# A two-pass attention layer: float32r parts for the query and key projections, 17-column values, and three steps of the slot plan moved

## The reference, cut to what matters

```python
qk = x @ W_attn + b_attn                       # queries and keys, 256 -> 512
y  = causal_attn(q, k, v=x)                    # first pass
e  = v[1:] - y[:-1]                            # second pass: values are what y missed
k2 = x[:-1] @ W_k2 + b_k2
y2 = causal_attn(q[1:], k2, e), one row of zeros put ahead
x  = layernorm(x + (y @ W_proj + b_proj) + (y2 @ W_proj + b_proj))
x  = layernorm(x + ffn(x))                     # experts touch only the first 512 rows
```

## Time and profile before

| | us |
|---|---|
| median of 3 runs | 2620.78 (2616.14 to 2626.06) |
| the profiled execution | 2615.51 |
| its span | 2613.8 |
| PE busy | 2477.4 (95%) |
| DVE busy | 2123.0 (81%) |
| ACT busy | 1763.8 (67%) |
| POOL busy | 1397.3 (53%) |

### The profile page before, as it was taken

One profiled execution on the slowest core, in us unless ns is written; L12 is line 12 of the kernel. 1 busy time (PEld: TensorE's weight loads), 2 busy tenths in 40 slices (PEclk: granted clock), 3 DMA queues, 4 the chain that ended last, 5 costly groups with the idle time before them and its releaser, 6 DMA issues.

```text
span 2613.8 us, 64356 instructions
## 1 busy us (share of the span) xinstructions
PE 2477.4 (95%) x19286; PEld 1215.6 (47%) x19286; DVE 2123.0 (81%) x9392; ACT 1763.8 (67%) x3388; POOL 1397.3 (53%) x2214
## 2 busy tenths in 40 slices
PE   3999999999999999999999999999999999999997
PEld 1444444444444444444444444444444444444444
DVE  2788888888888888888888888888888888888755
ACT  0377777677777766777777677777776777777652
POOL 2355555555555555555555555555555555555432
PEclk8699999999999999999999999999999999999999
DMA  5455555565555546555555565555556555554211
GB/s 96 87 105 87 93 94 101 98 116 103 104 92 95 101 91 111 108 106 95 93 96 97 103 116 103 101 91 94 103 90 115 104 107 95 92 100 86 67 53 52
DMA packets 187779, 251.18 MB, mean 96 GB/s; under 512 B 26769, under 2 KB 103193, under 8 KB 187417
## 3 DMA queue, kind: packets, MB, share of 16 engines
q1 hardware_dynamic: 187440, 247.07, 51.7%
HBM read 74.60 MB, written 16.78 MB: 35 GB/s over the span
## 4 chain that ended last, share of the span: by engine, by line
PE 79%; issue 7%; DVE 6%; ACT 5%; POOL 3%; SPq 1%; DMA 1%; ACTq 0%; POOLq 0%; DVEq 0%
PE score_t L627 22%; PE out_t L588 21%; PE misc L692 14%; PE score L638 9%; PE misc L727 5%; PE turn L670 5%; DVE junk L820 3%; ACT prob L498 2%; PE score L775 1%; ACT y_t L530 1%; PE misc L714 1%; POOL prob L422 1%; DVE resid L871 1%; PE score L791 1%; DVE max_cols L820 1%
## 5 line engine op out<-in xcount | busy, mean ns | idle before, releaser
L820 DVE CUSTOM_DVE_ANT_0 junk<-score,mask_rows 128x384 bf16<-128x384 f32 (+3 forms) x3584 | 1689.6, 514 | 378.5 <-PE score L638 374.8
L498 ACT ACTIVATE prob<-score_t 128x512 f32<-128x512 f32 x2560 | 1403.6, 598 | 614.4 <-PE score_t L627 609.6
L422 POOL TENSOR_SCALAR_AFFINE_SELECT prob<-prob 128x512 f32<-128x512 f32 (+1 forms) x1280 | 726.5, 569 | 1046.2 <-ACT prob L498 1046.1
L627 PE MATMUL score_t<-stack_q,stack_k 50*128 50x128 f32 (+5 forms) x4096 | 1052.7, 364 | 45.0 <-ACT prob L498 34.0
L638 PE MATMUL score<-stack_k,stack_q 48*128 48x512 f32 (+3 forms) x4096 | 1040.1, 352 | 9.8 <-DMA stack_q<-part_l 7.7
L627 PEld LDWEIGHTS score_t<-stack_q,stack_k 50*128 50x128 f32 (+1 forms) x4096 | 600.7, 185 | 778.2 <-ACT prob L498 673.3
L588 PE MATMUL out_t<-prob,value 128*32 128x512 f32 (+3 forms) x8192 | 711.3, 442 | 0.0
L638 PEld LDWEIGHTS score<-stack_k,stack_q 48*128 48x128 f32 x4096 | 607.8, 188 | 27.2 <-DVE max_cols L820 16.0
L692 PE MATMUL misc<-x_t,wq 128*128 128x512 f32 x512 | 285.4, 641 | 60.8 <-DMA bias<-L_attn_b_proj 31.3
L820 DVE DVE_READ_ACCUMULATOR2_ANT max_cols<- 128x1 f32 x4096 | 337.2, 82 | 0.0
L588 PEld LDWEIGHTS out_t<-prob,value 128*32 128x32 f32 x8192 | 187.5, 108 | 312.3 <-issue 215.1
(11 more groups left out here) (83 smaller groups left out, 1233.7 us busy)
## 6 DMA issues: line engine op xcount, KB each, us to landing
stack_k<-part_h SPq DMA_DIRECT2D x512, 128.0 KB, 4.2
stack_k<-part_l SPq DMA_DIRECT2D x256, 128.0 KB, 4.5
stack_q<-part_h SPq DMA_DIRECT2D x256, 128.0 KB, 4.1
x_t<-x_turned SPq DMA_DIRECT2D x32, 512.0 KB, 9.5
x_in<-L_attn_x SPq DMA_DIRECT2D x32, 512.0 KB, 14.1
stack_q<-part_l SPq DMA_DIRECT2D x128, 128.0 KB, 5.1
resid<-L_attn_x SPq DMA_DIRECT2D x32, 512.0 KB, 6.2
layer_out<-resid SPq DMA_DIRECT2D x31, 512.0 KB, 5.4
```

The lines of the kernel that those rows point to most:

```text
L422: e.affine_select(out=view, in_=view, compare_op=ALU.is_ge, fill=0.0, base=-unit_parts(unit)[1], pattern=[[0, runs], [0, cut], [1, P]], ch ...
L498: e.activation(prob[pair % RING][:, slot % 2 * 512:slot % 2 * 512 + 512], score_t[time % KEY_DEPTH][:, :], ACT.Exp, scale=1.0 / np.sqrt(HE ...
L627: done = e.matmul(score_t[now % KEY_DEPTH][:, col:col + n], keys[rows, pair, kb * P:(kb + 1) * P], stack_q[b % 2][rows, pair, kb * P:token ...
L820: e.tensor_tensor_reduce(junk[count % JUNK][:, 0:n], score[number % MAX_DEPTH][:, col:col + n], mask, 1.0, -3e38, ALU.add, ALU.max, max_co ...
```

## The change

Four things are changed, and nothing of what is computed:

1. The six pieces are made of float32r parts. The weights are loaded as float32 into space that `prob` uses later, and DVE splits them at the start into high and low parts (four operations), for which PE's first piece waits. x is loaded into one float32 tile `x_full`, and POOL splits it, per 128 channels, into high and low at slots 4 and 7 of place 6 (four operations a batch, after the mask and the piece's own split in each slot). Each L692 matmul becomes three float32r matmuls (high by high, low weights by high x, high weights by low x). There is one `x_t` instead of two, so the split of a batch waits until the last piece of the batch before is made, and the load of the next x waits for the split.
2. Value tiles are 17 columns wide instead of 32, and each L588 matmul writes 17 rows of its strip. `out_t` is cleared once at the start, so that the rows that are never written are defined.
3. ACT copies turned y one slot earlier, at (1, 3) and (2, 3), behind the `heads_t` copy of that slot.
4. The norm is applied at slots 3, 5, 7 and 9 of place 5, and the output's DMA goes from (6, 0) to (6, 1).

The core of the diff:

```diff
-        wq = sb("wq", [P, halves, 2 * halves, P])
-        wk2 = sb("wk2", [P, halves, halves, P])
+        wq = [sb(f"wq_{part}", [P, halves, 2 * halves, P], F32R) for part in "hl"]
+        wk2 = [sb(f"wk2_{part}", [P, halves, halves, P], F32R) for part in "hl"]
...
-        value1 = sb("value1", [P, blocks, HEADS, 32])
-        value2 = sb("value2", [P, blocks, HEADS, 32])
+        value1 = sb("value1", [P, blocks, HEADS, HEAD_DIM + 1])
+        value2 = sb("value2", [P, blocks, HEADS, HEAD_DIM + 1])
...
-            e.dma_start(x_t[1][:, :, :], x_turned[1].rearrange("(h p) t -> p h t", p=P)).then_inc(s_xt[1], 16)
...
-                if (place, slot) == (0, 8) and 2 <= b < batches:
-                    e.wait_ge(s_piece, N_PIECES * (b - 1))
-                    e.dma_start(x_t[b % 2][:, :, :], x_turned[b].rearrange("(h p) t -> p h t", p=P)).then_inc(s_xt[b % 2], 16)
+                if (place, slot) == (0, 8) and 1 <= b < batches:
+                    e.wait_ge(s_xsplit, 2 * halves * b)
+                    e.dma_start(x_full[:, :, :], x_turned[b].rearrange("(h p) t -> p h t", p=P)).then_inc(s_xt, 16)
...
-                if (place, slot) == (6, 0) and 1 <= b < batches:
+                if (place, slot) == (6, 1) and 1 <= b < batches:
...
+                for c in range(halves):
+                    b = ahead + 2
+                    if (place, slot) == (6, (4, 7)[c]) and 0 <= b < batches:
+                        if c == 0:
+                            e.wait_ge(s_xt, 16 * (b + 1))
+                            if b:
+                                e.wait_ge(s_piece, N_PIECES * b)
+                        e.tensor_copy(x_t[HIGH][:, c, :], x_full[:, c, :]).then_inc(s_xsplit, 1)
+                        e.wait_ge(s_xsplit, 2 * (halves * b + c) + 1)
+                        e.tensor_tensor(x_t[LOW][:, c, :], x_full[:, c, :], x_t[HIGH][:, c, :].bitcast(F32),
+                                        ALU.subtract).then_inc(s_xsplit, 1)
...
-                    if (place, slot) == ((1, 4), (2, 4))[hf] and 0 <= ahead - 1 < batches:
+                    if (place, slot) == ((1, 3), (2, 3))[hf] and 0 <= ahead - 1 < batches:
...
-                if place == 5 and slot in (1, 3, 5, 7) and 0 <= b < batches:
-                    apply_norm(e, b, slot // 2, x1_routed if b == 0 else resid, resid)
+                if place == 5 and slot in (3, 5, 7, 9) and 0 <= b < batches:
+                    apply_norm(e, b, slot // 2 - 1, x1_routed if b == 0 else resid, resid)
...
-                    done = e.matmul(out_t[32 * h:32 * h + 32, first:first + count], value[:, kb, GROUP * g + h, :],
+                    done = e.matmul(out_t[32 * h:32 * h + HEAD_DIM + 1, first:first + count], value[:, kb, GROUP * g + h, :],
...
-                        w = wk2[:, c, hf, :] if kind == "k2" else wq[:, c, hf + (0 if kind == "q" else halves), :]
-                        done = e.matmul(misc[:, :], w, x_t[b % 2][:, c, :], start=(c == 0), stop=(c == halves - 1))
+                        for i, (pw, px) in enumerate(zip(PARTS_K, PARTS_Q)):
+                            w = wk2[pw][:, c, hf, :] if kind == "k2" else wq[pw][:, c, hf + (0 if kind == "q" else halves), :]
+                            done = e.matmul(misc[:, :], w, x_t[px][:, c, :], start=(c == 0 and i == 0),
+                                            stop=(c == halves - 1 and i == TERMS - 1))
...
+            e.memset(out_t[:, :], 0.0).then_inc(s_ones, 1)
...
+            for i, (parts, full) in enumerate(((wq, wq_full), (wk2, wk2_full))):
+                e.tensor_copy(parts[HIGH][:, :, :, :], full[:, :, :, :]).then_inc(s_wsplit, 1)
+                e.wait_ge(s_wsplit, 2 * i + 1)
+                e.tensor_tensor(parts[LOW][:, :, :, :], full[:, :, :, :], parts[HIGH][:, :, :, :].bitcast(F32),
+                                ALU.subtract).then_inc(s_wsplit, 1)
```

More of the change, by code:

```diff
@@ L104, in build_layer @@
         ones = nc.alloc_sbuf_tensor_at("ones", [2 * MAX_PARTS, pairs, tokens], F32R, offset=prob_at)
-        value1 = sb("value1", [P, blocks, HEADS, 32])
-        value2 = sb("value2", [P, blocks, HEADS, 32])
+        wq_full = nc.alloc_sbuf_tensor_at("wq_full", [P, halves, 2 * halves, P], F32, offset=prob_at + 4 * pairs * tokens)
+        wk2_full = nc.alloc_sbuf_tensor_at("wk2_full", [P, halves, halves, P], F32, offset=prob_at + 5 * pairs * tokens)
+        value1 = sb("value1", [P, blocks, HEADS, HEAD_DIM + 1])
+        value2 = sb("value2", [P, blocks, HEADS, HEAD_DIM + 1])
         x_in = sb("x_in", [P, blocks, width])
@@ L112, in build_layer @@
         y_t = sb("y_t", [P, halves, tokens])
-        x_t = [sb(f"x_t{i}", [P, halves, tokens]) for i in range(2)]
+        x_full = sb("x_full", [P, halves, tokens])
+        x_t = [sb(f"x_t_{part}", [P, halves, tokens], F32R) for part in "hl"]
         heads_t = sb("heads_t", [P, tokens])
@@ L141, in build_layer @@
         s_weights, s_rows, s_next, s_resid, s_out = (sem(f"s_{n}") for n in ("weights", "rows", "next", "resid", "out"))
-        s_x, s_xt = sem("s_x"), [sem(f"s_xt{i}") for i in range(2)]
+        s_x, s_xt = sem("s_x"), sem("s_xt")
         s_stack = {(kind, hf): sem(f"s_stack_{kind}{hf}") for kind in ("q", "k", "k2") for hf in range(halves)}
         s_maxrow = [sem(f"s_maxrow{i}") for i in range(2)]
-        s_const, s_ones, s_bias = (sem(f"s_{n}") for n in ("const", "ones", "bias"))
+        s_const, s_ones, s_bias, s_wsplit = (sem(f"s_{n}") for n in ("const", "ones", "bias", "wsplit"))
         s_key, s_qry, s_pv, s_turned, s_piece, s_yt_pe, s_proj, s_neg_pe = (
@@ L155, in build_layer @@
             sem(f"s_{n}") for n in ("max", "negl", "value1", "den", "rden", "normal", "attended", "stats", "aggr"))
-        s_mask, s_split, s_value2, s_added, s_biased, s_ln = (
-            sem(f"s_{n}") for n in ("mask", "split", "value2", "added", "biased", "ln"))
+        s_mask, s_split, s_xsplit, s_value2, s_added, s_biased, s_ln = (
+            sem(f"s_{n}") for n in ("mask", "split", "xsplit", "value2", "added", "biased", "ln"))
         s_fin, s_fbias = sem("s_fin"), sem("s_fbias")
@@ L286, in _ @@
         def _(e):
-            e.dma_start(x_t[0][:, :, :], x_turned[0].rearrange("(h p) t -> p h t", p=P)).then_inc(s_xt[0], 16)
-            e.dma_start(wq[:, :, :, :], w_attn.rearrange("(h p) (w n) -> p h w n", p=P, n=P)).then_inc(s_weights, 16)
+            e.dma_start(x_full[:, :, :], x_turned[0].rearrange("(h p) t -> p h t", p=P)).then_inc(s_xt, 16)
+            e.dma_start(wq_full[:, :, :, :], w_attn.rearrange("(h p) (w n) -> p h w n", p=P, n=P)).then_inc(s_weights, 16)
             e.dma_start(bias_qk[:, :], b_qk).then_inc(s_weights, 16)
-            e.dma_start(wk2[:, :, :, :], w_k2.rearrange("(h p) (w n) -> p h w n", p=P, n=P)).then_inc(s_weights, 16)
+            e.dma_start(wk2_full[:, :, :, :], w_k2.rearrange("(h p) (w n) -> p h w n", p=P, n=P)).then_inc(s_weights, 16)
             R, M = SCORE_ROWS, MAX_PARTS
@@ L576, in _ @@
             e.wait_ge(s_const, 11)
+            e.wait_ge(s_ones, 3)
             def weigh(unit, kb, first, count, start=False, stop=False):
@@ L680, in _ @@
                                 e.wait_ge(s_weights, WEIGHTS)
+                                e.wait_ge(s_wsplit, 4)
                             if n % N_PIECES == 0:
-                                e.wait_ge(s_xt[b % 2], 16 * (b // 2 + 1))
+                                e.wait_ge(s_xsplit, 2 * halves * (b + 1))
                             if n:
```

## The result

| | before | after |
|---|---|---|
| median us | 2618.46 (4 runs) | 2544.69 (2539.26 to 2552.98, 4 runs) |
| ratio of after to before | | 0.972 (95% interval 0.968 to 0.975) |
| profiled execution, its span | 2615.51, 2613.8 | 2552.98, 2551.2 |

The change makes the kernel 2.8% faster. The forecast was 2512 us, in a range of 2476 to 2570: the direction and the range hold, but of the 109 us that the prediction summed up, 74 came. The profiled execution is the slowest of the four.

The account below looks back on a forecast made before the run. The prediction took PE as the bound, busy for all but 0.5 us of each place or less. Terms of 1.68 + 0.15 + 1.36 + 0.29 = 3.48 us a batch, times 31, plus 1 at the start, gave 2512 us, range 2476 to 2570.

Parts of the forecast that it names:

- The rival of shown weight loads: Projection blocks: each float32r matmul's weight load shows, a block stays at 1.06 us; 2565 us in all, chance 0.13.
- that of two passes: Projection blocks: a float32r matmul on the whole array takes two passes, a block 1.52 us; 2735 us in all, chance 0.05.
- first failed step: Places 0, 1, 2 and 7: eight projection blocks save 0.19 us each, 1.5 a batch, as DVE has a margin.
- The term of 0.03 for late exps at slot 9: Slot-9 blocks: the next exps come within 0.1 us of being late, so 0.03 us is taken off the saving.
- Place 4: nothing: Place 4: block savings count for 0, as DVE is busy 10.58 of 10.62 us from its first maximum there.
- 0.5 us of each place or less: All eight places of a steady batch: PE is busy for all but 0.5 us of each or less.
- 0.68 twice: Places 1 and 2: the earlier copy of y saves 0.61 us of wait plus 0.07 of first load, 1.36 a batch.
- 0.29 a batch: Places 5 and 6: the later norm's net gain, 0.44 us less 0.15, with 0.19 counted under the projection blocks.
- the 0.44: Place 5, slot 7: of 0.52 + 0.19 us only 0.44 shows, as PE's value block needs POOL's mask.
- 0.15 taken: Value blocks: 17-column weight loads save 0.3 us a batch, or 0 with a floor; 0.15 is taken.
- this rival: Places 6 and 7: POOL's overflow of 1.4 to 1.6 us shows as PE waiting for masks; 2562 us, chance 0.12.
- what is next?: Places 1 and 2, earlier copy of y: scores of slots 6 and 7 need two exps, done 0.3 us or more before.

Follow-up runs that it names:

- experiment 5: DVE's normalisation of a unit's heads moved from slot 6 to slot 8, on top of experiment 1; 2504.03 us, ratio 0.956 to the kernel before.
- Experiment 7: One more POOL subtraction in each half of the split of x in place 6, on top of experiment 1; 2630.16 us, ratio 1.005 to the kernel before.
- experiment 1: Load of `resid` moved from slot 8 of place 1 to slot 4 of place 0 in the changed kernel; 2521.62 us, ratio 0.9625 to the kernel before.

## Why the prediction was right where it was, and where it was not

- **The block.** Its rate was taken from the scores of rows 4, and the rate holds on 128 rows: 0.23 a matmul (0.222 forecast), 0.90 a block (0.87). The saving was 0.16 instead of 0.19. The rival of shown weight loads (0.32 a matmul) and that of two passes (0.44) fall by the starts 1041.57 and 1041.80. By a rule of the Trainium skill ("TensorE: Matmul & The Clock Gate", Part 3, "The mechanism") loads would not overlap here, since all three matmuls use all rows; the trace disagrees, and the measurement decides. That section of the Trainium skill also has loads into a background weight buffer pulled ahead of running matmuls, which the prediction left aside and which would fit these starts; no run shows such a buffer.
- **Where it counts.** This was the first failed step: "eight blocks, 8 x 0.19 = 1.5, as DVE has a margin there". A margin over a whole place says nothing about slot 9. DVE does its normalisation and four maxima back to back there, and the second score pair, which needs the maxima of slot 8, comes 0.11, 0.12 and 0.17 us later than before in places 0, 1 and 5. In place 6 it is 0.12 later without part 4, and 0.04 with it, where the exps are late as well. The term of 0.03 for late exps at slot 9 is the only one that the prediction had for such a wait, on another engine and too small. Parts 1 and 2 gave 47 us, not 57.
- **Places 4 and 5.** "Place 4: nothing" holds as a sum: place 4 got 0.16 shorter, and the value block of slot 1 in place 5 starts at 1.13 instead of 0.96. (PE's idle time in place 5 before is 0.56 us, a little over the "0.5 us of each place or less"; nothing was built on that.)
- **The copy of y.** 0.68 twice, 42 us forecast, 43 measured alone.
- **The norm.** 0.29 a batch forecast, 0.35 measured (11 us by the places, 14 by the medians). The gain in place 5 is a little under the 0.44. The late exps of place 6, for which 0.15 was taken off, are there (experiment 5), and place 6 came out at the 7.8 of the forecast. But part 1 alone costs that place the same 0.16 by DVE, and the two waits overlap, so part 4 adds nothing to it. The place was right with one of its two causes unseen, which is partly luck.
- **17 columns.** 0.15 taken, 8 us measured alone, near the full 0.3 (9 us). The 13 ns a load show in the trace.
- **POOL.** The sum of durations up to the mask of slot 9 was right: within 0.1 us of the deadline, and 0.10 measured. Experiment 7 shows that a little more would have made this rival the outcome.
- **What was missing.** The second failed step is an omission. Part 3 asks "what is next?" and looks at ACT and PE alone. The bias addition on POOL in place 2 waits for a load whose time doesn't shrink with the places. Before, no row showed it, since a wait that is covered leaves none. Over 26 batches, in medians: before, the addition starts 7.9 us after the load's issue, and the load has landed 1.6 us ahead of it. The copy of y alone makes the first 6.9 and leaves 0.7; parts 1 and 2 alone keep it at 8.1, but the landing goes from 6.3 to 7.2 us and leaves 0.8. With all parts the landing takes 8.0, and nothing is left. So about half of the margin went with the shorter places and half with a slower landing. Why it lands later was not tested; the load of x ahead of it takes longer too (11.1 us after, 9.7 before), and by the medians it lands 2.4 us after the load of `resid` is issued, where it was 0.6. Cost: 23 us by experiment 1. With this step the sum would have been 2512 + 23 = 2535, and with 47 instead of 57 us for parts 1 and 2, 2545.
- **The range.** It held, but by room that was meant for something else: its upper end of 2570 stood for shown weight loads and for POOL as the limit, and neither came. What used the room, the late load and DVE at slot 9, was not among the rivals. That the number lies inside is in that part luck.

## What to carry to other kernels

When stages get shorter, list every transfer that is issued a fixed number of slots ahead, and compare its time to landing with the new distance; the profile before shows no wait for a load that is just in time. Read an engine's margin at the slot where the other engine comes for the result, not as busy time over a whole stage. And price a saved wait or matmul only up to the next engine that is already back to back: here the first 0.16 us of each of twelve blocks (1.9 us) were worth some 1.2 us a batch, and the next 0.23 (2.8 us) 1.1.

## What the runs showed of the hardware

- A wait of PE of about 2 us can cost more than itself, and doesn't always. In 29 of 30 batches of experiment 7 PE waits 1.95 to 1.97 us for a mask in place 7. In 7 of them the granted clock stays full and the place takes 11.64 us. In the others matmuls of 512 columns stand 0.43 us apart for a while afterwards, half the clock, and the place takes 12.6 to 14.7 us. In the changed kernel the same happened in place 3, in 2 of 32 batches. The second window here is one of them, the first a batch at full clock:

```profile
1215.01:1228.55 13.54, 11.77 (x86) 6.61 (x86) 8.76 (x41) 6.88 (x14) 9.01 (x12) 1.00 0.45 70
...
2172.76:2187.78 15.02, 13.25 (x86) 6.97 (x85) 8.84 (x41) 6.97 (x14) 9.07 (x12) 0.89 0.41 64
```

PE waits 1.78 us for the mask in the first and 1.77 in the second. Against 10.94 with the early load, the late load costs 2.6 us in the first; in the second 1.5 us of clock come on top. So the clock is some 3 us in two batches, of the 23 that the late load costs in all. Why the four runs of the changed kernel lie 14 us apart (7 us in experiment 1) is open: the fastest has the highest mean granted clock (0.998) and the slowest the lowest (0.982), but the two between are out of order, and it was not tested.

- A chain of float32r matmuls on all 128 rows, each with its own 128 columns of weights, runs at 0.23 us per 512 columns; three of them (0.90) cost less than one float32 matmul of the same size (1.06).

- A weight load of 17 columns is 12 to 13 ns shorter than one of 32: by its record (96 and 108 ns) and by the distance from a value block to the next scores (0.988 and 1.001 us), and the kernel gets 8 us faster by it.
